# Two-layer metaformer kernel: statistics and powers for the next layer's first groups at other units of the MoE stage, and an exponential's table load there

## The reference, cut to what matters

```python
x = x + conv0(layernorm(x))
gate = silu(einsum('nd,edh->enh', t, W_gate)); up = einsum('nd,edh->enh', t, W_up)
routed = einsum('ne,end->nd', combine, einsum('enh,ehd->end', gate * up, W_down))
x = x + shared(t) + routed            # t = layernorm(x), 8 experts of 64, top 2, and a shared one
```

## Time and profile before

| what | value |
|---|---|
| runs of the kernel before | 438.13, 439.88, 440.44 us; median 439.88 |
| the profiled execution's own time | 439.87 us |
| its span, first to last instruction | 438.0 us |
| mean granted TensorE clock (of full speed) | 0.867 |
| busy: TensorE, VectorE, GpSimd, ScalarE | 361.0, 273.2, 172.6, 152.1 us |
| power on GpSimd, line 159 | 10 in all, 1807 ns each |
| GpSimd's product, line 806 | 48, 1017 ns each |

### The profile page before, as it was taken

The page is one execution under the profiler, slowest core; times in us unless marked ns, Lnnn a source line. Parts: engine busy times, 40 slices in busy tenths (PEclk is TensorE's granted clock), DMA queues, the critical chain, the costliest instruction groups (busy, mean ns, idle before and its releaser), DMA issues.

```text
span 438.0 us, 6363 instructions
## 1 busy us (share of the span) xinstructions
PE 361.0 (82%) x2077; PEld 306.4 (70%) x2077; DVE 273.2 (62%) x892; ACT 152.1 (35%) x324; POOL 172.6 (39%) x188
## 2 busy tenths in 40 slices
PE   5955858967999999996477999999889785899880
PEld 5955857956888888883367999998789651793330
DVE  5836894861343343385365676867674779259997
ACT  3220163444333333331224455584553620340000
POOL 5750141003488557455000852100135666005773
PEclk9999555569999999998556799999999978699996
DMA  8940410006449455520111101111001011872335
GB/s 183 273 135 6 140 76 1 1 6 151 113 106 358 104 133 198 171 47 1 28 27 28 27 8 35 35 35 35 0 13 44 24 37 49 291 259 64 91 103 150
DMA packets 29455, 39.30 MB, mean 90 GB/s; under 512 B 4504, under 2 KB 24793, under 8 KB 29150
## 3 DMA queue, kind: packets, MB, share of 16 engines
q1 hardware_dynamic: 24910, 32.05, 26.8%
q0 software_dynamic: 1728, 3.54, 2.6%
q10 hardware_dynamic: 2784, 3.29, 2.2%
HBM read 22.92 MB, written 12.93 MB: 82 GB/s over the span
## 4 chain that ended last, share of the span: by engine, by line
PE 26%; POOL 8%; DVE 7%; issue 4%; ACT 4%; DMA 3%; POOLq 0%; SPq 0%; DVEq 0%; ACTq 0%
PE ps L1771 6%; POOL xn L1177 4%; PE ps L1739 3%; PE ps L1912 3%; PE ps L1751 2%; POOL wide L1177 2%; DVE mx L1236 2%; POOL slots L1146 2%; PE ps L1924 2%; PE ps L1758 1%; DVE K L1251 1%; PE ps L1721 1%; PE ps L1720 1%; PE ps L1719 1%; PE ps L1790 1%
## 5 line engine op out<-in xcount | busy, mean ns | idle before, releaser
L806 POOL TENSOR_TENSOR t<-wide,wstage 128x384 f32<-128x384 f32 x48 | 48.7, 1017 | 69.5 <-DMA wide<-combine_w 38.1
L927 DVE TENSOR_TENSOR h<-ps,t 128x384 f32<-128x384 f32 x48 | 26.8, 558 | 57.6 <-POOL t L806 57.5
L159 POOL TENSOR_TENSOR rstd<-sm,neg_half 128x9 f32<-128x9 f32 x10 | 18.0, 1807 | 112.3 <-DVE sm L153 112.3
L844 PE MATMUL ps<-wide,gu_w 128*128 128x384 f32 x108 | 50.9, 471 | 2.9 <-PEq L713 1.7
L900 ACT ACTIVATE wstage<-ps 128x384 f32<-128x384 f32 (+1 forms) x60 | 29.4, 489 | 66.0 <-PE ps L846 63.3
L1771 PE MATMUL ps<-V,wide 128*128 128x129 f32 x400 | 52.1, 279 | 0.0
L868 PE MATMUL ps<-h,wd 128*128 128x384 f32 x120 | 49.4, 494 | 2.9 <-DVE h L927 2.5
L1771 PEld LDWEIGHTS ps<-V,wide 128*128 128x128 f32 x400 | 49.1, 194 | 0.1
L1815 PE MATMUL ps<-ew,xTd 128*128 128x512 f32 x72 | 37.3, 655 | 3.6 <-DVE R L1484 3.5
L1484 DVE SCALAR_TENSOR_TENSOR R<-ps,dense_w,R 128x128 f32<-128x128 f32 x144 | 38.3, 343 | 1.2 <-PE ps L1815 1.1
L1236 DVE TENSOR_REDUCE mx<-ps 128x1 f32<-128x576 f32 (+1 forms) x40 | 29.8, 749 | 13.6 <-PE ps L1739 13.4
(11 more groups left out here) (248 smaller groups left out, 780.1 us busy)
## 6 DMA issues: line engine op xcount, KB each, us to landing
wide<-combine_w SPq DMA_DIRECT2D x24, 384.0 KB, 5.5
slots<-zrow SPq DMA_DIRECT2D x7, 768.0 KB, 7.1
xe<-slots SPq DMA_DIRECT2D x16, 192.0 KB, 3.9
slots<-wide ACTq DMA_DIRECT2D x16, 192.0 KB, 2.9
xall<-in_x SPq DMA_DIRECT2D x8, 288.0 KB, 6.1
out<-R SPq DMA_DIRECT2D x9, 192.0 KB, 2.2
Q<-sQK SPq DMA_DIRECT2D x8, 144.0 KB, 2.4
K<-sQK SPq DMA_DIRECT2D x8, 144.0 KB, 2.5
```

Source lines behind the costliest of these rows:

```text
L806: nc.gpsimd.tensor_tensor(t4[v % 2][:], cB[c % 2][:, u % NB2, :], s4[u % 2], ALU.mult).then_inc(t_ok, 1)
L844: nc.tensor.matmul(o, gu_w[0][:, w], xTH[:, at], start=True, stop=False)
```

## The change

The six steps with statistics move from units 50 to 55 to units 36 to 41. The three steps that apply the norm move from units 56 to 58 to units 45 to 47. The two powers move from behind GpSimd's loop to behind its product in units 41 and 46. The memsets that stood in these units go to later ones. The wait for the six finished chunks of `R` moves from unit 50 to unit 36. On ScalarE an exponential of one element into `once` is added behind `silu(59)`.

```diff
+        STATS_AT, RSTD_AT, NORM_AT = 36, (41, 46), 45
...
-                    elif v > 8 and v - 9 < len(firsts):
-                        ap, value = firsts[v - 9]
+                    elif u in RSTD_AT:
+                        g = RSTD_AT.index(u)
+                        pool.wait_ge(var5, g + 1)
+                        norm_rstd(GT, g, P, rs5)
+                    elif v > 8 and z.n < len(firsts):
+                        ap, value = firsts[z.n]
...
-                for g in range(BEFORE):
-                    pool.wait_ge(var5, g + 1)
-                    norm_rstd(GT, g, P, rs5)
...
                     if u + 1 < UNITS:
                         silu(u + 1)
+                    elif u + 1 == UNITS:
+                        nc.scalar.activation(once[0:1, :], konst[0:1, K_ID:K_ID + 1], ACT.Exp)
...
-                    if UNITS - 2 * NB2 <= u < UNITS:
-                        if u == UNITS - 2 * NB2:
-                            dve.wait_ge(R_ok, CHUNKS // 2)
-                        ahead(u - UNITS + 2 * NB2)
+                    if u == STATS_AT:
+                        dve.wait_ge(R_ok, CHUNKS // 2)
+                    if u - STATS_AT in range(6):
+                        ahead(u - STATS_AT)
+                    if u - NORM_AT in range(3):
+                        ahead(u - NORM_AT + 6)
```

More of the change, by code:

```diff
@@ L813, in _ @@
                         z.wait()
-                assert len(firsts) <= 39
+                assert z.n == len(firsts)
                 z.wait()
-                for g in range(BEFORE):
-                    pool.wait_ge(var5, g + 1)
-                    norm_rstd(GT, g, P, rs5)
             @block.sync
```

## The result

The changed kernel takes 436.51 us, the median of 20 runs, against 440.62 for 20 runs of the kernel before. Two of the 20 runs of the changed kernel fell in a slower state; the ratio of the others to the kernel before is 0.9902, 95% interval 0.9876 to 0.9927: 4.3 us faster, where 5.3 were forecast. The prediction was right in sign and range, and 1 us too good. The profiled execution has a span of 434.6 us, 3.4 less than before.

The account below looks back on a forecast made before the run. TensorE was taken to bound the MoE stage, a chain of short steps the seam. Gains of 5.26 and 0.82 less 0.74 lost gave 5.34, from 439.87 to 434.5 us; own range 433 to 436.5, whole range 431.0 to 437.4.

Parts of the forecast that it names:

- The end without the wait, 5.26 us: MoE stage's tail: last `down` starts 0.06 behind last `hidden`, copy at 202.48 instead of 207.74; 5.26 us gained.
- The clock, 0.82: Seam: three transposes behind the copy and the next stage's first three run at full clock; 0.82 us gained.
- The statistics, 0.88 lost: Unit 38's moments delay shared unit 39's `hidden`, so TensorE's second gate matmul of unit 41 comes 0.88 us later.
- The powers, 0.1 lost: GpSimd's powers behind the products of units 41 and 46: nearly hidden, 0.1 us lost.
- The 0.24 that came back: Statistics' old place: that chunk took 8.52 against 8.28, so moving them gains 0.24 us.
- The table: Load moved from the first exponential to behind the last silu, done before the copy is wanted: nothing counted.
- What comes behind: After 210 everything runs 5 us earlier; clock return could gain up to some 4 us or lose 1.5.
- The signs of being wrong: Unit 46's chunk longer too, line 948 over 0.4 us an instruction, or first transposes 5 us earlier but the end not.
- (a): Clock returns early behind the seam: 3 us more gained, 431.5 us; chance 0.08.
- (b): Table's drain or a late clock takes part of the gain: 435.7 us by the drain; chance 0.05.
- (c): Powers not hidden, GpSimd the bound in units 41 and 46: 3.6 us lost, 438.1 us; chance 0.06.
- (d): Units 45 to 47: nine norm instructions each wait for a GpSimd product, 9.1 us; 443 us, slower; chance 0.04.

Follow-up runs that it names:

- the table load alone: Kernel before plus only the one-element exponential behind the last silu; one run 442.71 us, beside 438.37 to 443.35 for the kernel before.
- powers alone: Changed kernel with statistics and norm steps back at their old units, powers at units 53 and 56; 438.18 us, ratio 0.9927 to the kernel before.
- the kernel placed for the shared units: Changed kernel with statistics in units 35, 36, 37, 40, 41, 42 and powers in 43 and 48; 436.25 us, ratio 0.9897 to the kernel before.

## Why the prediction was right, point by point

- **The wait for the power was on the path**: right. It is gone, and it was worth about 4.0 us of the tail (4.26 - 0.24). The path I followed (power, three norm steps, three `hidden`, `down`, copy) was the one that set the end.
- **The end without the wait, 5.26 us**: the mechanism was right, this term was mis-sized. I let the last `down` start 0.06 behind the last `hidden`. That is what happens when `hidden` is late. After the change TensorE still has the rest of one `down` and two whole ones in its own queue when the last `hidden` ends, since `down` runs three units behind `feed`: the `hidden` ends at 202.49 and the last `down` at 204.14, 1.65 later, where I had 0.97. Counted from the start of the last chunk, the tail became 14.97 - 10.24 = 4.73 shorter. The 0.24 that the old statistics had cost in front of unit 56 is in it, so the term measured 4.5 in place of 5.26: 0.77 too much.
- **The clock, 0.82**: the three transposes behind the copy took 0.55 for 0.90, and the first six of the next stage 0.85 for 1.51. The first part came out at 0.35 instead of 0.41, and the level held for the second. So at the first transpose my sum stood at 5.26 + 0.41 - 0.74 = 4.93, against 4.14 measured. But the table load alone got the same 0.55 and 0.85 with the wait still there. The term is a matter of where the clock falls in an execution, and it should have been in the range, not in the sum.
- **The statistics, 0.88 lost**: 0.73 measured, at the place named. The step with moments took 2.24 between two `hidden` and not 2.39: the 2.39 that I took from the kernel before had a held instruction in it (last section).
- **The powers, 0.1 lost**: 0.23, at the place and by the way named. The memset of 1.38 was the right nearest row for its being nearly hidden, not for all of it.
- **The 0.24 that came back**, and the net of 0.74 lost in the chunks: 0.73 + 0.23 - 0.24 = 0.72. The parts were off by 0.15 and 0.13 in opposite directions, so that the net fits this well is luck.
- **The table**: no cost and no gain, as forecast. The one-element exponential started 0.01 behind the load (201.77 + 1.28 = 203.05, start at 203.06). By an estimate from the drain that the Trainium skill gives (ScalarE: Activation LUTs, What ACT_TABLE_LOAD costs) it would have ended 1.4 us later, at 204.6, behind the time at which the copy was wanted; the trace shows no drain.
- **What comes behind**: the clock came back 35 us behind the first transposes, 36 before. The third power, for the next layer's third group, starts 32.76 us behind the first transposes before and 32.54 after, so the gain was carried on that far. From the first transposes to the end it took 227.9 us before and 228.4 after, and 226.0 to 231.3 in all the profiles; with the 0.23 ahead of the change that is why the two spans differ by 3.4 and not by 4.14. In the experiments the distance to the third power ranges from 30.6 to 32.9 with the same code behind the seam, 2 us that belong to no edit; the whole times of one kernel spread over about 5 us (437.90 to 442.89 before).
- **The signs of being wrong**: two of the three that I had named came, and the forecast held all the same. The chunk with unit 46 was longer too (8.51), but the 0.23 arise at the start of unit 46 itself, by the first power: `feed(46)` waits for `hidden(44)`, so my own path for the 0.1 already led into that chunk, and the sign was badly chosen. And a norm instruction took over 0.4 us (0.95 and 0.46); that cost nothing that the steps show.
- **Rivals**: the early return of the clock (a) did not come: the level came back only in the window from 241 to 242, and the short return before 236 of the earlier trace rows was gone. No part of the drain (b) showed. Powers not hidden (c) fell, except for 0.23. The slower one (d) had its mechanism in the trace, but not its price: see the last section. The one that I had not written down, a power that waits for its moments with products behind it, costs 1.9 us when it is built (powers alone, 12.82 - 10.71 - 0.24 = 1.87); the change avoids it by its distance of three and five units.

## What to carry to other kernels

When a wait is removed from the tail of a pipelined loop, ask what the engine behind it has still queued: the new end is the later of the data's arrival and the engine's own backlog, here 1.65 us of `down`. Work moved into a steady loop is free only where a unit's slack is; look for the unit at which the engine that sets the pace waits for the one that takes the extra work. Here it is the shared unit, in which GpSimd has no product and VectorE must be prompt: GpSimd's extra work belongs right in front of it, VectorE's away from it. A request that waits on its input belongs so late in a queue that it never waits, since everything behind it waits too.

## What the runs showed of the hardware that I had not expected

Some of VectorE's instructions are held by GpSimd's product, but not by its power: in these traces those that read two tensors in the on-chip memory SBUF, and the TENSOR_SCALAR form. `hidden`, one of whose tensors is TensorE's output outside SBUF, took its 0.56 at 184.25 with products running from 183.09 to 185.09, and three `bn_stats`, which read one tensor, their 0.67 at 164.47 beside a product from 164.54. Five rows of the changed kernel's timeline:

```profile
174.56 1.08 DVE L147 TENSOR_TENSOR sm<-sm 128x9 f32<-128x9 f32 x1
...
180.36 1.02 POOL L808 TENSOR_TENSOR t<-wide,wstage 128x384 f32<-128x384 f32 x1 [0.49 <-DVE h L932]
...
180.51 0.95 DVE L953 TENSOR_SCALAR xn<-R,sm,rstd 128x128 f32<-128x128 f32 x1
...
181.34 1.80 POOL L159 TENSOR_TENSOR rstd<-sm,neg_half 128x9 f32<-128x9 f32 x1
...
182.36 0.86 DVE L953 TENSOR_SCALAR xn<-R,sm,rstd 128x128 f32<-128x128 f32 x3
```

The 128x9 instruction of line 147 takes 168 to 170 ns all ten times in the kernel before, and 1.08 us here: it began at 174.56, two hundredths before the product of 174.58 to 175.62 (the row above, in the chunk of unit 40), and ended with it. The first norm instruction started at 180.51 inside the product of 180.36 to 181.38, took 0.95 instead of 0.34, and ended 0.08 behind the product. The next group, at 182.36, lay beside the power of 181.34 to 183.14 but for its last 0.08 and took its 0.86 for three. That product reads two large tensors; the power works on 128x9 elements for 1.80 us. In the kernel placed for the shared units, where all three groups meet a product, the groups take 1.31, 1.21 and 1.30 us, the longest single instruction 0.80, and the chunk steps stay at 8.28. The Trainium skill (SBUF — State Buffer, Who interferes with whom) states an exclusive lock; these traces agree for the product and disagree for the power. A group is held for the rest of one product (0.35 to 0.46 us there, 0.61 in the first group of the changed kernel), and not once an instruction: GpSimd had no next product to slip in between, which is where rival (d) failed. Why the power holds nothing was only seen, not tested.

The hold was already in the trace of the kernel before, in the moments of unit 52; the rows that the prediction went by showed nothing beside a product only because they held no such instruction:

```profile
190.74 1.02 POOL L806 TENSOR_TENSOR t<-wide,wstage 128x384 f32<-128x384 f32 x1 [0.67 <-ACT wstage L900]
...
191.38 0.41 DVE L143 TENSOR_TENSOR sm<-st 128x9 f32<-128x9 f32 x1
```

The same instruction takes 0.17 at 168.56 in the changed kernel, where no product runs; here it ends 0.03 behind the product. A memset holds less: beside the one from 175.69 to 176.32 in the changed kernel the TENSOR_SCALAR of line 153 took 0.37 for 0.17, while line 150, which reads two tensors, took its 0.17.
